# Two kinds of small TensorE products moved within the steps of a fused decoder, one of them into another PSUM bank

## The chip, the core and the metric

The kernel runs on one core of a Trainium2 chip, as one launch. The metric is the time of the launch on the device in microseconds (us); less is better. Before the change three runs took 360.64, 361.13 and 362.26 us, so the median is 361.13 us.

## What is computed

Two decoder layers over x of 16 x 64 tokens with 128 features, all in float32. After each of the six blocks the input is added and a layer norm without weights is made:

```python
x = _layernorm(x + L0_attn(x))          # 16 heads of 8, rotary positions, causal, biases
x = _layernorm(x + L0_xattn(x, ctx))    # 16 heads of 8, keys and values from ctx, mask, biases
x = _layernorm(x + L0_ffn(x))           # 8 experts of 512, the best 2 of each token, silu(g) * u
x = _layernorm(x + L1_attn(x))          # 16 heads of 64, no mask
x = _layernorm(x + L1_xattn(x, ctx))    # 16 heads of 8, mask
x = _layernorm(x + L1_ffn(x))           # ternary weights, 512 wide, gelu, layer norm, projection
# one attention: q, k, v = x @ Wq, src @ Wk, src @ Wv, cut into heads
#   att = softmax(q k^T / sqrt(d) + mask);  out = (att v) @ Wo
```

## The kernel before

The 1024 tokens are eight tiles of 128 rows (two sequences of 64). The three attentions with heads of 8 are objects of class Narrow: a0 (self-attention with rotary positions, "rope"), a1 and a2 (cross-attentions). The attention with heads of 64 is `wide`, the last block is `fc`, the experts are `moe`. The tiles stand in two streams: `pre` is a0's eight and then a1's eight (places 0 to 15), `post` is wide's, a2's and fc's (places 0 to 23; a2 has 8 to 15). Between the streams lie a drain written out by hand, in which the last tiles of a1 end while the experts' weights are turned, and the experts' 23 blocks.

Four functions write each engine's program, one step j after the other, and a step works on several tiles at once, each at another stage of its way. In a step of narrow tiles TensorE does, in this order: the scores of tile j-2 (`s_pe`, L539 and L547 or L550), the transpose of the normalized y of tile j-5 (`y_pe`, L582), the projections of k and q of tile j (`qk_pe`, L511), the value projection of tile j-2 (`v_pe`, L523), the transposes of P, the exponentials, of tile j-3 (`t_pe`, L429), the output projection of tile j-5 (`o_pe`, L586), P's products with the values of tile j-4 (`va_pe`, L566), and the transpose of the finished X of tile j-6 (`x_pe`, L371). I call the tile that is transposed at the end of step j "X of step j". TensorE has no other order than this one: each product waits by semaphores for its inputs and for the readers of the PSUM bank that it writes.

Three shapes of the array are used, and the profile prints them with each product: 128\*128 (the whole array: projections and transposes), 128\*64 (the value projection and P's products with values) and 64\*64 (the scores).

The other engines in such a step: ScalarE (ACT) copies y (`y_act`, L632 or L630), q (`qk_act`), the values (`v_act`, L620, two copies), P transposed (`pt_act`, L438, two copies), makes the exponentials (`exp_act`, L419) and copies X transposed into XT (`x_act`, L376). VectorE (DVE) makes the row maximum (L403) and the difference (L413), the residual and its statistics (L388, L324, L326), k, and then the reciprocals and ysb (L676, L680). GpSimd (POOL) spreads k into blocks (KB, L690), makes the norm's root (L331, L333), applies it (L337) and adds a bias (L716).

Banks of PSUM that matter here: B_S (two, scores), B_PT (two, P transposed), B_Y (P's products with values in columns 0 to 287, and the value projection in 384 to 511), B_OX (y transposed, output projection, X transposed), B_K and B_Q (k and q of a tile, 128 columns each). No product is written into a bank while an engine reads another part of it; the waits see to that.

At the first block of the experts TensorE first does 32 transposes whose result is not used (`turn_over`, L1521), then the first block that the DMA queue of SyncE (SP) has loaded into XG (`block_pe`, L1527). At the start of `post`, VectorE combines the experts' outputs of a pair of tiles (`combine`) and applies their norm (`apply`, L1742), and TensorE turns them (`turn_pe`, L1752).

## Time and profile before

| what | value |
|---|---|
| median of three runs | 361.13 us |
| the profiled execution, its own time | 360.73 us |
| its span (first to last instruction) | 358.7 us |
| busy in the span: PE | 321.0 us (89%) |
| PEld, DVE, ACT, POOL | 262.9 us, 231.4 us, 182.5 us, 203.0 us |
| mean granted TensorE clock, share of full speed | 0.983 |

The page of the profile gives, for each engine, its busy time, and then the chain of work that ended last, followed back from the last instruction. The timeline lists instructions in the order of time, with neighbours of one kind merged: start, the time from the first start to the last end, the line, what is written and read, the shape of the array for products, and the count (one product of float32 is two entries). In brackets stands how long the engine had been idle before, and what released it. Because products overlap in the pipeline, it is the distance from one start to the next that tells what a group costs TensorE, and not its printed length.

### The profile page before, as it was taken

To read this page: it belongs to the slowest core of one execution; us is meant where nothing else is said; L and a number is where in the kernel's file an instruction comes from. 1 tells how busy PE (TensorE), PEld (TensorE's weight loads), DVE (VectorE), ACT (ScalarE), POOL (GpSimd) and SP (SyncE) were. 2 spreads that over 40 slices of the span, in tenths; PEclk is the share of its full clock that TensorE was granted. 3 is DMA by queue.
4 is the path that set the end of the run, shared out by engine and by line. 5 is a ranking of instruction groups with operands and counts; after the bars stand their busy time and mean duration, and the time that the engine had idled before them with its cause. 6 is when DMAs were issued, how large, how long until landed. Compare 5 with 4: busy or idle time off the path is not lost.

```text
span 358.7 us, 10785 instructions
## 1 busy us (share of the span) xinstructions
PE 321.0 (89%) x4214; PEld 262.9 (73%) x4214; DVE 231.4 (65%) x554; ACT 182.5 (51%) x384; POOL 203.0 (57%) x289
## 2 busy tenths in 40 slices
PE   2969999999888799999994689999999799999993
PEld 2647667777677799999994567788888577767673
DVE  2698987887876033583343479765556667877685
ACT  2457667776658732333322234445444466667651
POOL 2756998887677335553314776432122564576784
PEclk9998999999999999999999699999999999999998
DMA  6799999100011111111101110000000000000001
GB/s 190 219 308 246 296 324 322 32 2 3 16 38 47 59 41 50 46 45 51 41 22 36 40 38 24 2 4 2 2 4 2 3 4 3 2 2 2 4 22 37
DMA packets 37052, 23.55 MB, mean 66 GB/s; under 512 B 4228, under 2 KB 34956, under 8 KB 36876
## 3 DMA queue, kind: packets, MB, share of 16 engines
q1 hardware_dynamic: 35692, 20.16, 19.9%
q0 software_dynamic: 1024, 2.10, 2.0%
q8 instruction: 34, 0.56, 0.7%
q10 hardware_dynamic: 288, 0.62, 0.5%
q14 instruction: 14, 0.11, 0.1%
HBM read 15.13 MB, written 7.73 MB: 64 GB/s over the span
## 4 chain that ended last, share of the span: by engine, by line
PE 74%; DVE 12%; issue 4%; ACT 4%; POOL 3%; DMA 2%; SPq 1%; POOLq 0%; ACTq 0%; DVEq 0%
PE banks L429 8%; PE banks L801 8%; PE banks L1555 6%; PE banks L1586 6%; PE banks L1563 6%; PE banks L566 5%; PE banks L539 5%; PE banks L845 4%; PE banks L813 4%; PE banks L511 3%; PE banks L861 2%; PE banks L523 2%; PE banks L827 2%; PE banks L1026 2%; ACT WALL L1353 2%
## 5 line engine op out<-in xcount | busy, mean ns | idle before, releaser
L690 POOL TENSOR_TENSOR KB<-KT,cst 128x512 f32<-128x512 f32 x48 | 49.3, 1048 | 8.1 <-DVE KT L650 5.8
L438 ACT ACTIVATE PT<-banks 128x512 f32<-128x512 f32 x64 | 34.8, 595 | 24.4 <-PE banks L429 23.2
L403 DVE TENSOR_REDUCE mx<-banks 128x16 f32<-128x1024 f32 x32 | 38.6, 1206 | 11.7 <-PE banks L550 10.1
L1578 DVE TENSOR_TENSOR PT<-banks,PR 128x512 f32<-128x512 f32 x23 | 15.9, 691 | 40.2 <-PE banks L1563 35.9
L1543 POOL COPY U<-WALL 128x1024 f32 x21 | 21.9, 1042 | 34.8 <-PE banks L1563 34.7
L877 ACT ACTIVATE U<-banks 128x512 f32<-128x512 f32 x44 | 26.1, 597 | 29.7 <-PE banks L801 14.4
L331 POOL TENSOR_SCALAR ve<-mv 128x1 f32<-128x1 f32 x40 | 9.2, 231 | 49.4 <-DVE mv L326 49.0
L429 PE MATMUL banks<-cst,PR 128*128 128x128 f32 x256 | 35.4, 282 | 0.6 <-POOL PR L906 0.6
L419 ACT ACTIVATE PR<-PR 128x1024 f32<-128x1024 f32 x32 | 33.8, 1058 | 3.6 <-DVE PR L413 3.3
L801 PE MATMUL banks<-XT,WQKV 128*128 128x128 f32 x256 | 32.1, 286 | 0.4 <-ACT XT L1758 0.4
L801 PEld LDWEIGHTS banks<-XT,WQKV 128*128 128x128 f32 x256 | 30.6, 199 | 1.1 <-ACT XT L1758 0.7
L429 PEld LDWEIGHTS banks<-cst,PR 128*128 128x128 f32 x256 | 28.1, 143 | 4.3 <-POOL PR L906 1.5
L413 DVE TENSOR_TENSOR PR<-banks,mx 128x1024 f32<-128x1024 f32 x24 | 29.4, 1224 | 0.8
L539 PE MATMUL banks<-KB,QS 64*64 64x512 f32 x192 | 27.0, 627 | 3.2 <-DVE PR L413 2.2
L566 PE MATMUL banks<-VB,PT 128*64 128x18 f32 x768 | 26.7, 212 | 0.0
L566 PEld LDWEIGHTS banks<-VB,PT 128*64 128x64 f32 x768 | 24.3, 138 | 3.0 <-issue 0.5
L1712 POOL DMA_INDIRECT KB<-routed_rows,pos x16 | 15.9, 993 | 16.4 <-DMA routed_rows<-YS 12.3
L333 POOL TENSOR_TENSOR rstd<-ve,half 128x1 f32<-128x1 f32 x40 | 23.2, 579 | 3.3
L1586 PE MATMUL banks<-WALL,PT 128*128 x184 | 24.4, 276 | 0.6 <-DVE YS L1594 0.6
L1555 PE MATMUL banks<-XGT,U 128*128 128x128 f32 x184 | 24.5, 276 | 0.5 <-ACT XGT L1533 0.5
L906 POOL TENSOR_TENSOR PR<-PR,rs 128x1024 f32<-128x1024 f32 x8 | 15.2, 1904 | 17.1 <-DVE rs L916 17.0
L1563 PE MATMUL banks<-XGT,U 128*128 128x128 f32 x184 | 24.3, 275 | 0.0
(192 smaller groups left out, 727.0 us busy)
## 6 DMA issues: line engine op xcount, KB each, us to landing
routed_rows<-zero SPq DMA_DIRECT2D x1, 4544.0 KB, 19.7
WALL<-in_L_ffn_wg_dram SPq DMA_DIRECT2D x8, 256.0 KB, 5.5
WALL<-in_L_ffn_wu_dram SPq DMA_DIRECT2D x8, 256.0 KB, 5.7
WALL<-in_L_ffn_wd_dram SPq DMA_DIRECT2D x8, 256.0 KB, 6.1
U<-in_L_attn_W_qkv_dram SPq DMA_DIRECT2D x1, 1536.0 KB, 22.2
XG<-routed_rows SPq DMA_DIRECT2D x23, 64.0 KB, 1.8
routed_rows<-YS SPq DMA_DIRECT2D x23, 64.0 KB, 1.6
cst<-shape_constants ACTq DMA_DIRECT2D x1, 537.0 KB, 4.4
```

The costliest lines, as they stand in the source:

```text
L403: dve.tensor_reduce(mx[:, n % 2, :], s, AX.X, ALU.max).then_inc(self.max.sem, 1)
L413: dve.tensor_tensor(PR[:, n % 2, :].rearrange("q (h k) -> q h k", k=SEQ), s, bc(mx[:, n % 2, :], 2, SEQ), ALU.subtract).then_inc(self.sub. ...
L419: act.activation(p, p, ACT.Exp, scale=self.scale).then_inc(self.exp.sem, 1)
L429: t = pe.transpose(PS[:, B_PT + m, P * (r % 4):P * (r % 4 + 1)], PR[:, n % 2, P * r:P * (r + 1)], ident)
L438: act.activation(PT[:, n % 2, 4 * m:4 * m + 4, :].rearrange("p r q -> p (r q)"), PS[:, B_PT + m, :], ACT.Copy).then_inc(self.pt.sem, 1)
L539: pe.matmul(PS[q, B_S + g, :], QS[f, n % 3, q], KB[f, n % 2, b].rearrange("p h k -> p (h k)"), start=True, stop=False)
L566: m = pe.matmul(PS[64 * b:64 * b + 64, B_Y, w * r:w * (r + 1)], PT[:, n % 2, r, 64 * b:64 * b + 64], VB[:, n % 3, r, b].rearrange("p a e - ...
L690: pool.tensor_tensor(KB[:, n % 2, b], bc(KT[:, n % 2, b, :], 1, 8), bc(cst[:, C_HEAD:C_HEAD + 8], 2, SEQ), ALU.mult).then_inc(self.kb.sem, 1)
L801: m = pe.matmul(PS[:, bank, P * k:P * (k + 1)], WQKV[:, f // 2, P * u:P * (u + 1)], XT[:, P * i:P * (i + 1)], start=True, stop=True)
L1555: m = pe.matmul(PS[:, j % 2, P * c:P * (c + 1)], WE[:, j % 3, 0, P * c:P * (c + 1)], XGT[:, j % 3, :], start=True, stop=True)
L1563: m = pe.matmul(PS[:, 2 + j % 2, P * c:P * (c + 1)], WE[:, j % 3, 1, P * c:P * (c + 1)], XGT[:, j % 3, :], start=True, stop=True)
L1586: m = pe.matmul(PS[:, 7, 0:P], HT[:, j % 2, c, :], WALL[:, e, 2, P * c:P * (c + 1)], start=(c == 0), stop=(c == CH - 1))
```

## The change

It has four parts.

1. **Value projection.** For a narrow tile that has a narrow tile two places behind it in the stream (`late_v`: places 0 to 13 of `pre`, a2's places 8 to 13 of `post`) v_pe is written into bank B_Q, columns 128 to 255, and stands right ahead of va_pe, after o_pe. It waits for q's copy of the tile of this step (`after2 ... qk_read`), because that copy reads the same bank, and the projection of q three tiles on waits for v's copy. va_pe no longer waits for v's copy. On ACT v_act comes after pt_act. The first ranking product of the experts (`rank_pe`, in B_Q) waits for the v of place 13.
2. **X.** For a0's tiles, a1's first and a2's places 8 to 13 (`late_x`) the transpose of X is taken from the end of a step and stands in the next step between s_pe and y_pe; its copy on ACT comes after y_act. y_pe no longer waits for the copy of X two tiles back, and o_pe does.
3. **turn_over** does 25 transposes in place of 32.
4. **apply** for tiles 2 to 5 of the experts' norm comes on DVE after max_dve, ahead of the copies of wide's projections, and not after them.

```diff
 qk_pe:
                 for bank, w, src, s in ((B_K, 1, self.src, self.k_mm), (B_Q, 0, XT, self.q_mm)):
+                    if s is self.q_mm and job.ago(3) and job.ago(3).late_v:
+                        for r in job.ago(3).v_read():
+                            pe.wait_ge(*r)
...
+            def v_at(self, job, rows, b):
+                bank, c = (B_Q, P) if job.late_v else (B_Y, 384)
+                return PS[rows, bank, c:c + P] if b is None else PS[rows, bank, c + 64 * b:c + 64 * b + 64]
 v_pe:
-                if job.ago(3):
+                if job.late_v:
+                    pe.wait_ge(*job.after2.stage.qk_read(job.after2.i)[1])
+                elif job.ago(3):
                     pe.wait_ge(*job.ago(3).y_read())
...
-                        m = pe.matmul(PS[64 * a:64 * a + 64, B_Y, 384 + 64 * b:448 + 64 * b],
+                        m = pe.matmul(self.v_at(job, slice(64 * a, 64 * a + 64), b),
 va_pe:
-                if job.after2:
+                if job.after2 and not job.after2.late_v:
 y_pe:
-                if job.ago(2) and not (self is a1 and i >= 6):
+                if job.ago(2) and not job.ago(2).late_x and not (self is a1 and i >= 6):
 o_pe:
+                if job.ago(2) and job.ago(2).late_x:
+                    pe.wait_ge(*job.ago(2).x_read())
...
+            def late_v(self):
+                return isinstance(self.stage, Narrow) and self.after2 is not None
+            def late_x(self):
+                return self.late_v and not (self.stage is a1 and self.i >= 1)
 stream_pe:
                 if y:
+                    if y.ago(2) and y.ago(2).late_x:
+                        y.ago(2).stage.x_pe(pe, y.ago(2))
                     y.stage.y_pe(pe, y)
...
-                if a:
+                if a and not a.late_v:
                     a.stage.v_pe(pe, a)
...
                 if y:
                     y.stage.o_pe(pe, y)
+                if a and a.late_v:
+                    a.stage.v_pe(pe, a)
                 if v and not first_v and not v.stage.wide:
                     v.stage.va_pe(pe, v)
...
                 for x in turned(tiles, j):
-                    x.stage.x_pe(pe, x)
+                    if not x.late_x:
+                        x.stage.x_pe(pe, x)
 stream_dve:
                     v.stage.max_dve(dve, v)
+                if tiles is post and j in (2, 3):
+                    for g in (2 * j - 2, 2 * j - 1):
+                        moe.apply(dve, g)
 Routed.pe:
-                self.turn_over(pe, 32)
+                self.turn_over(pe, 25)
 post_dve:
-            if not late and j in (2, 3):
-                for t in (2 * j - 2, 2 * j - 1):
-                    moe.apply(dve, t)
```

TensorE in a step of a1, before. L539 and L550 are the scores, L371 is X of the step before or of this one.

```order
L539 MATMUL banks<-KB,QS 64x512 x4
L550 MATMUL banks<-mrb,fills 64x512 x4
L582 MATMUL banks<-cst,ysb 128x128
L511 MATMUL banks<-CT,WT 128x128
L511 MATMUL banks<-XT,WT 128x128
L523 MATMUL banks<-WT,CT 64x64 x4
L429 MATMUL banks<-cst,PR 128x128 x8
L586 MATMUL banks<-WT,yT 128x128
L566 MATMUL banks<-VB,PT 64x18 x16
L371 MATMUL banks<-cst,X 128x128
```

The same step now (the scores have the lines L548 and L559, y L591, k and q L514, v L532, the output projection L597, P's products with values L575).

```order
L548 MATMUL banks<-KB,QS 64x512 x4
L559 MATMUL banks<-mrb,fills 64x512 x4
L371 MATMUL banks<-cst,X 128x128
L591 MATMUL banks<-cst,ysb 128x128
L514 MATMUL banks<-CT,WT 128x128
L514 MATMUL banks<-XT,WT 128x128
L429 MATMUL banks<-cst,PR 128x128 x8
L597 MATMUL banks<-WT,yT 128x128
L532 MATMUL banks<-WT,CT 64x64 x4
L575 MATMUL banks<-VB,PT 64x18 x16
```

The value projection has moved behind the output projection, and X ahead of y; the array changes its shape before each of L582, L523, L429, L566, L371 and L539 in the first list, and before L371, L532 and L548 in the second.

TensorE in `post` from step 11 on, where the last two tiles of `wide` meet a2: the end of L845, wide's output projection (128\*64), to the next scores, before.

```order
L845 MATMUL banks<-U 64x128
L429 MATMUL banks<-cst,PR 128x128 x8
L371 MATMUL banks<-cst,X 128x128
L539 MATMUL banks<-KB,QS 64x512 x4
L550 MATMUL banks<-mrb,fills 64x512 x4
```

And now.

```order
L429 MATMUL banks<-cst,PR 128x128 x8
L532 MATMUL banks<-WT,CT 64x64 x4
L371 MATMUL banks<-cst,X 128x128
L548 MATMUL banks<-KB,QS 64x512 x4
L559 MATMUL banks<-mrb,fills 64x512 x4
```

Here the value projection, which stood ahead of L845 and had its shape, has moved between two groups of 128\*128. This is so in steps 10 and 11 of `post`.

VectorE in step 2 of `post`, before: L403 and L409 are the maximum and the difference of wide's first tile, L877 copies of its projections, L1742 is `apply`, L1722 the start of `combine`.

```order
L403 TENSOR_REDUCE mx<-banks 128x16
L409 TENSOR_TENSOR PR<-banks,mx 128x2x8x64
L877 COPY U<-banks 128x512 x2
L1742 TENSOR_SCALAR X<-R,mv,rstd 128x128 x2
L1722 SCALAR_TENSOR_TENSOR R<-KB,pk,X 128x128
```

And now.

```order
L403 TENSOR_REDUCE mx<-banks 128x16
L409 TENSOR_TENSOR PR<-banks,mx 128x2x8x64
L1777 TENSOR_SCALAR X<-R,mv,rstd 128x128 x2
L888 COPY U<-banks 128x512 x2
L1757 SCALAR_TENSOR_TENSOR R<-KB,pk,X 128x128
```

The two `apply` have changed places with the two copies, and stand directly behind the difference.

## Rows read from the trace of the kernel before

**Rows 1.** Page, part 4: the chain that ended last, by engine.

```profile
PE 74%; DVE 12%; issue 4%; ACT 4%; POOL 3%; DMA 2%; SPq 1%; POOLq 0%; ACTq 0%; DVEq 0%
```

**Rows 2.** Timeline of PE, one step of a1: start, length, line, shapes, count.

```profile
60.95 1.09 PE L539 MATMUL banks<-KB,QS 64*64 64x512 f32 x8
61.85 0.40 PE L550 MATMUL banks<-mrb,fills 64*64 64x512 bf16 x4
62.18 0.33 PE L582 MATMUL banks<-cst,ysb 128*128 128x128 f32 x1
62.35 0.39 PE L511 MATMUL banks<-CT,WT 128*128 128x128 f32 x2
62.57 0.39 PE L511 MATMUL banks<-XT,WT 128*128 128x128 f32 x2
62.89 0.45 PE L523 MATMUL banks<-WT,CT 128*64 128x64 f32 x8
63.27 1.09 PE L429 MATMUL banks<-cst,PR 128*128 128x128 f32 x8
64.20 0.39 PE L586 MATMUL banks<-WT,yT 128*128 128x128 f32 x2
64.52 1.11 PE L566 MATMUL banks<-VB,PT 128*64 128x18 f32 x32
65.56 0.33 PE L371 MATMUL banks<-cst,X 128*128 128x128 f32 x1
65.82 1.09 PE L539 MATMUL banks<-KB,QS 64*64 64x512 f32 x8
```

**Rows 3.** Timeline of PE: a step without X, and a long run of one shape.

```profile
34.16 1.11 PE L566 MATMUL banks<-VB,PT 128*64 128x18 f32 x32
35.20 1.09 PE L539 MATMUL banks<-KB,QS 64*64 64x512 f32 x8
...
112.91 5.00 PE L1348 MATMUL banks<-cst,WALL 128*128 128x128 f32 x44
```

**Rows 4.** Timeline of all engines in the step of rows 2.

```profile
62.29 1.23 DVE L403 TENSOR_REDUCE mx<-banks 128x16 f32<-128x1024 f32 x1 [0.88 <-PE banks L550]
...
63.00 0.37 ACT L609 ACTIVATE QS<-banks,qkb 128x128 f32<-128x128 f32 x1
...
65.00 1.06 ACT L419 ACTIVATE PR<-PR 128x1024 f32<-128x1024 f32 x1
...
65.61 0.23 POOL L331 TENSOR_SCALAR ve<-mv 128x1 f32<-128x1 f32 x1 [0.52 <-DVE mv L326]
```

**Rows 5.** Timeline of DVE, a step of a0 (rope).

```profile
43.37 1.23 DVE L413 TENSOR_TENSOR PR<-banks,mx 128x1024 f32<-128x1024 f32 x1
...
44.71 0.29 DVE L388 TENSOR_TENSOR R<-banks,XR 128x128 f32<-128x128 f32 x1
```

**Rows 6.** Timeline of PE at the first block of the experts; and XG's landings.

```profile
119.68 3.68 PE L1521 MATMUL banks<-cst 128*128 128x128 f32 x32 [1.77 <-ACT WALL L1353]
123.20 0.27 PE L1527 MATMUL banks<-cst,XG 128*128 128x128 f32 x1
```

```profile
DMA to landing us min/median/max: 1.7/1.8/3.1
```

**Rows 7.** Timeline of all engines, steps 2 and 3 of post.

```profile
213.81 0.59 DVE L1742 TENSOR_SCALAR X<-R,mv,rstd 128x128 f32<-128x128 f32 x2
...
214.50 0.41 PE L1752 MATMUL banks<-cst,X 128*128 128x128 f32 x2 [1.35 <-issue]
...
222.27 1.09 PE L429 MATMUL banks<-cst,PR 128*128 128x128 f32 x8 [0.63 <-POOL PR L906]
```

**Rows 8.** Timeline of PE, step 11 of post, and of DVE in step 12.

```profile
298.46 0.29 PE L845 MATMUL banks<-WOUT,U 128*64 128x128 f32 x1 [0.56 <-ACT U L877]
```

```profile
304.82 1.23 DVE L413 TENSOR_TENSOR PR<-banks,mx 128x1024 f32<-128x1024 f32 x1
```

**Rows 9.** Timeline of PE, step 19 of post.

```profile
334.35 0.30 PE L582 MATMUL banks<-cst,ysb 128*128 128x128 f32 x1 [0.54 <-issue]
```

More of the change, by code:

```diff
@@ L620, in v_act @@
                     m = act.activation(VB[rows, n % 3, :, :, a, 0:DH].rearrange("p r b d -> p b r d"),
-                                       PS[rows, B_Y, 384:512].rearrange("p (b r d) -> p b r d", b=2, d=DH), ACT.Copy)
+                                       self.v_at(job, rows, None).rearrange("p (b r d) -> p b r d", b=2, d=DH), ACT.Copy)
                 m.then_inc(self.v_ready.sem, 1)
@@ L1218, in stream_act @@
                     y.stage.y_act(act, y)
+                    if y.ago(2) and y.ago(2).late_x:
+                        y.ago(2).stage.x_act(act, y.ago(2))
                 b, q, v = at(tiles, j), at(tiles, j - 1), at(tiles, j - 2)
@@ L1229, in stream_act @@
                     v.stage.vw_copies(act, 0, v)
-                    v.stage.v_act(act, v)
+                    if not v.late_v:
+                        v.stage.v_act(act, v)
                 extra(act, j, False)
@@ L1234, in stream_act @@
                     t.stage.pt_act(act, t)
+                if v and v.late_v:
+                    v.stage.v_act(act, v)
                 hidden = v and isinstance(v.stage, Ternary)
@@ L1244, in stream_act @@
                 for x in turned(tiles, j):
-                    x.stage.x_act(act, x)
+                    if not x.late_x:
+                        x.stage.x_act(act, x)
                 extra(act, j, True)
@@ L1405, in rank_pe @@
                     pe.wait_ge(s_rt, 3)
+                    for s in pre[-3].v_read():
+                        pe.wait_ge(*s)
                 else:
```

2 lines of the change are left out of this document (added).

## The prediction, made before the changed kernel ran

> **What bounds the kernel now.** I read the chain that ended last first: 74% of the span is PE [rows 1]. So the question is which parts of the program PE sets, and for what it pays there. The timeline of PE answers it for a step of a1 [rows 2]: from 60.95 to 65.82 there is no bracket with idle time; one step takes 4.87 us, and the steps of a1 and a2 repeat it. The reader is to look there at the starts, and to compare them with what the same products cost in a row. 44 transposes of shape 128\*128 take 5.00 us, the last of them some 0.28, so 0.11 each [rows 3]. In rows 2 the eight of L429 take 63.27 to 64.20, 0.93 in place of 0.88; the two of L586 0.32 in place of 0.22; the second pair of L511 0.32 where the first took 0.22; X (L371) 0.26 in place of 0.11; y (L582) 0.17 in place of 0.11. The excess stands only where the shape of the array changes: some 0.10 behind the last product of the old shape and some 0.05 at the first of the new one. A semaphore is not its cause: L511's second operand, L429 and L586 all wait for something else than their forerunner, and between L429 and L586 there is none. A second reading gives the same without a model: with X between L566 and the next scores it is 1.30 us from 64.52 to 65.82 [rows 2], without it 1.04, from 34.16 to 35.20 [rows 3]; so an X alone among other shapes costs 0.26, and in a run of its own shape 0.11.
>
> Of the other engines I want the slack in the same step [rows 4]. DVE was idle for 0.88 before its maximum, POOL for 0.52 before the norm's root. So PE could be faster by about 0.5 before POOL sets the pace, and by 0.9 before DVE does.
>
> **The price of a step after the change.** A step has six changes of shape now and three then. (a) v joins L566: L511 to L566 took 3.21 us (62.35 to 65.56). Now L511 takes 0.44 and L429 0.88 without a change, L586 0.32 with the change behind it, v 0.28 (its 0.38 less the exit of 0.10), and L566 1.02, since v pays the entry. That is 2.94, or 0.27 less. (b) X joins y: 0.15. Together 0.42, and a step takes 4.45. POOL's 0.52 leaves 0.10, DVE's 0.88 leaves 0.46: PE stays the bound, POOL closely behind.
>
> The Trainium skill, page "TensorEngine Tiling (Array Packing)", Key Properties, says that changing the tiling mode drains the engine, and "TensorE: Matmul & The Clock Gate", Single matmul latency, puts a drain at about 128 cycles. At 2.4 GHz that would be an estimated 0.05 us for each change, 0.16 per step and not 0.42, and the forecast would be about 358 us (4.45 us of gain from (a) and (b) become 1.7). The rows above have 0.15 per change, and they decide.
>
> **New waits.** v waits for q's copy on ACT. That copy took 0.37 and ended at 63.37, 2.42 us into the step [rows 4]; the copy of X, of the same size, now comes ahead of it, so it ends at 2.8 at the latest. v now stands behind L429 and L586, at 1.23 (scores) + 0.06 + 0.11 (X) + 0.11 (y) + 0.44 + 0.88 + 0.32 = 3.15: it would wait for nothing, with 0.35 to spare. Queued behind it are L566 and the next scores, for which DVE waits. On ACT v's copies only change places with P's, so that the exponentials, which ended at 66.06 and so 5.1 into the step [rows 4], end 0.37 later for X's sake, at 5.5; L429 needs them 1.95 into the next step, that is at 6.4. o_pe's wait for X's copy (over at 2.45) ends before its turn (2.83). The three waits cost nothing; without that cover each costs what it overruns, in every step.
>
> **The sum**, in stretches.
>
> *a0's steps 4 to 7.* Here DVE has the rotary work too, and PE waits for it. The residual (44.71) starts 0.11 after the difference has ended (43.37 + 1.23) [rows 5], because it waits for PE's L586. With v out of the way L586 comes 0.4 earlier, and 0.1 of that is gained in each of steps 6 and 7; X doesn't matter there. Ahead of them step 4 and step 5 are PE's and POOL's, and I take 0.25 for v's part, less than one step's (a). Sum 0.4, bounds 0 and 0.9.
>
> *pre, from step 8 to step 16.* Part (a) holds in steps 8 to 15, 8 x 0.27 = 2.2. Part (b) holds at seven borders of steps, since a1's tiles 1 to 7 keep their X at the end: 7 x 0.15 = 1.05. Sum 3.2. If POOL can't follow at 4.45 the bound is its own 4.87 - 0.52 = 4.35 and some jitter; at the worst half of this stays, 1.6. The drain behind it is a chain from these tiles through DVE, ACT and POOL, all of which start from PE's last scores, so it moves as a whole and keeps the gain.
>
> *turn_over.* 32 transposes take 119.68 to 123.20, 0.11 each; seven fewer are 0.77, if the first block is there at 122.43. Its load was issued at 120.55 and a landing takes 1.7 to 1.8 us in the median [rows 6]: 122.3. I take 0.77; with the longest landing of 3.1 it would be 0.
>
> *apply.* Now the two norms (0.59 on DVE) stand where DVE would else wait for PE's products, and not between the last copy and combine. The chain goes combine, POOL's root, two gathers, POOL's shares, L429, which waited 0.63 for it [rows 7]. combine starts earlier by the two norms, 0.59, less their overlap with the copy ahead: 0.4. PE's own wait of 1.35 before L1752 goes too, but PE then waits longer at 222: nothing of it counts. Bounds 0 and 0.6.
>
> *Steps 10 to 12 of post.* Here the change costs. v stood ahead of L845, with its shape, and in the time that L845 waits for ACT anyway (0.56 [rows 8]). Now it stands between two groups of 128\*128: 0.24 for its four pairs of products, and 0.15 for the change of shape on either side, 0.53 in each of steps 10 and 11 (the exact starts in rows 2 give 0.10 + 0.38 + 0.05). Step 12 saves 0.28 again by (a), so that 0.8 is left if PE alone sets these steps. But DVE's difference of step 12 ends only at 306.05 (304.82 + 1.23) [rows 8], the scores of the next step wait for it, and its chain starts at L845 of step 11, ahead of the second 0.53. Half of the 0.8 would hide there; I take a loss of 0.45, bounds 0.2 and 1.1.
>
> *Steps 13 to 19 of post.* (a) in steps 13, 14 and 15, 0.8; (b) at the three borders of 14/15 to 16/17, 0.45. From step 18 on the scores are fc's, of shape 128\*128, and (b) gives nothing. In step 19 y waited 0.54 [rows 9], because X's copy two tiles back stood behind the table load and the gelu on ACT; y no longer waits for it, but the transposes behind y still wait for that gelu, so I take 0.35, bounds 0 and 0.5. Sum 1.6.
>
> 0.4 + 3.2 + 0.77 + 0.4 - 0.45 + 1.6 = 5.9. The profiled execution of 360.73 becomes 354.8. It was 0.4 faster than the median of the three, and from the median 361.13 it is **355.2 us**.
>
> **Rivals.** *POOL becomes the bound.* For it: only 0.10 is left of its 0.52, and the order of its work (root, norm, bias, KB) is a chain that starts from DVE's statistics. Against it: its blocks are needed only one step after they are made. If a step settles at 4.65, half of the 4.45 us that (a) and (b) bring (3.2 + 1.25) is lost: 357.4.
>
> *The gaps are not the shape's.* Then (a) and (b) give nothing, and the rest, 0.77 + 0.4 + 0.35 less 0.1 or 0.2, gives 359.8. Against it: the two readings of X, 1.30 and 1.04.
>
> *The change doesn't reach the end.* The drain or the start of post could be set by something that doesn't move with PE's steps, such as a DMA. Then up to 2 us are given back: 356.9. The drain's waits name DVE, ACT and POOL, so I hold this for small.
>
> *Slower: v waits for q's copy.* ACT's row y, X, q, P, v, exponentials would have to put q's copy later than v's turn. It starts to cost at 0.35 of delay and eats the step's gain from 0.35 + 0.42 = 0.77 us on. If the copy came 1.0 us late in each of some 18 steps, each would lose 0.2: 361.13 + 3.6 - 1.1 (the other terms) = 363.6. Against it: ACT's exponentials end about one us into the next step, while y's copy can't start before 1.6.
>
> **Chances.** Forecast with its bounds 0.74; POOL's pace 0.11; gains given back 0.07; gaps not the shape's 0.04; slower 0.04. The range takes in POOL's pace and, on the other side, all terms at their better ends (0.5 in a0, 0.2 in apply, 0.25 at steps 10 to 12, 0.15 at step 19, and some of each step): 353.6 to 357.6. About 0.5% (1.8 us) is what a measurement of this kernel can tell from no change: faster by more 0.92, within it 0.04, slower by more 0.04.
>
> **What would show it.** In the timeline of PE a step of a1 of 4.45 us without idle; 0.11 for each of X and y in a row; 1.04 or so from L575 to the scores. DVE idle for 0.46 and POOL for 0.1 before the same rows; a wait of PE on DVE's k, on KB or in front of L532 would show the rivals. L1527 2.75 us after the first of 25 transposes. L429 in step 3 of post still waiting for POOL. Two longer steps, 10 and 11, in post. The largest doubt is POOL's 0.10.

## The result, and the profile after

The changed kernel takes 358.16 us (median of 5 runs, 356.87 to 358.33), the kernel before 361.72 in the 5 runs beside it: a ratio of 0.9893, 95% interval 0.9864 to 0.9922. The change makes the kernel faster by about 1%, which is 3.6 us, where 5.9 were forecast; 358.2 lies outside the range of 353.6 to 357.6. In the later batches of runs the kernel before had medians of 360.95 to 361.12, against which the gain is 2.8 to 3.0 us. The profiled execution took 358.16 with a span of 356.2, and that of the kernel before 360.73 with 358.7: 2.5 us in the traces. The terms of the forecast are compared with this pair of traces.

Two rows of the page answer to [rows 1] and to the granted clock of the kernel before. First the chain that ended last, then PE's granted clock in 40 slices of the span (9 is 90% or more):

```profile
PE 69%; DVE 14%; ACT 5%; issue 5%; POOL 2%; DMA 2%; SPq 1%; POOLq 0%; ACTq 0%; DVEq 0%
PEclk9989999999999999999997699999999999999999
```

PE still sets most of the chain, five points less than before. The 7 and the 6 stand where the kernel before has a single 6: there the kernel runs at a lower clock for longer.

**A step of a1.** The timeline of PE (start, length, line, shapes, count), in the place of [rows 2]:

```profile
63.66 1.09 PE L548 MATMUL banks<-KB,QS 64*64 64x512 f32 x8
...
64.90 0.33 PE L371 MATMUL banks<-cst,X 128*128 128x128 f32 x1
65.07 0.27 PE L591 MATMUL banks<-cst,ysb 128*128 128x128 f32 x1
65.17 0.39 PE L514 MATMUL banks<-CT,WT 128*128 128x128 f32 x2
...
66.50 0.39 PE L597 MATMUL banks<-WT,yT 128*128 128x128 f32 x2
66.81 0.45 PE L532 MATMUL banks<-WT,CT 128*64 128x64 f32 x8
67.09 1.06 PE L575 MATMUL banks<-VB,PT 128*64 128x18 f32 x32
68.09 1.29 PE L548 MATMUL banks<-KB,QS 64*64 64x512 f32 x8
```

63.66 to 68.09 is 4.43 us, for which 4.45 was forecast; y takes 0.10 behind X, and the scores start 1.00 after L575. But the next L548 takes 1.29 in place of 1.09, and the step that begins with it 4.63. Between the first and the last step of a1 steps of 4.43 and 4.63 alternate. POOL in the same place (it answers to the last row of [rows 4]):

```profile
61.17 0.46 POOL L727 TENSOR_TENSOR XR<-X,rowb 128x128 f32<-128x128 f32 x1
61.58 2.04 POOL L701 TENSOR_TENSOR KB<-KT,cst 128x512 f32<-128x512 f32 x2
63.90 0.23 POOL L331 TENSOR_SCALAR ve<-mv 128x1 f32<-128x1 f32 x1 [0.27 <-DVE mv L326]
...
65.79 0.46 POOL L727 TENSOR_TENSOR XR<-X,rowb 128x128 f32<-128x128 f32 x1
66.21 2.05 POOL L701 TENSOR_TENSOR KB<-KT,cst 128x512 f32<-128x512 f32 x2
68.33 0.23 POOL L331 TENSOR_SCALAR ve<-mv 128x1 f32<-128x1 f32 x1
```

KB's second half ends at 66.21 + 2.05 = 68.26, after the start of the long L548 at 68.09; at 63.62 it was 0.04 ahead of the short one at 63.66. In the short row the first four of L548's products start within 0.02 us; in the long one the two that need KB's second half start 0.22 behind the other two, at 68.31. POOL's idle time is 0.27 in one step and none in the next, where [rows 4] have 0.52.

**The start of post.** Stretches of 3 us: busy time of PE, its weight loads, DVE, ACT and POOL, then the granted clock (0.84 in the first row of the changed kernel). First three of the kernel before, then five of the changed kernel:

```profile
196.00:199.00 3.00, 0.00 (x0) 0.00 (x0) 1.26 (x5) 0.00 (x0) 2.00 (x4) 0.56 0.19 44
199.00:202.00 3.00, 2.22 (x9) 1.96 (x10) 1.36 (x5) 0.28 (x1) 2.51 (x4) 0.50 0.13 30
202.00:205.00 3.00, 3.00 (x24) 3.00 (x24) 0.94 (x2) 1.58 (x3) 2.50 (x3) 0.80 0.17 44
```

```profile
190.00:193.00 3.00, 1.16 (x8) 0.97 (x8) 0.96 (x5) 0.00 (x0) 2.39 (x3) 0.84 0.17 46
193.00:196.00 3.00, 0.45 (x1) 0.18 (x1) 1.83 (x7) 0.04 (x1) 2.19 (x4) 0.50 0.16 41
196.00:199.00 3.00, 2.71 (x12) 2.72 (x13) 0.97 (x4) 0.78 (x2) 2.39 (x5) 0.50 0.17 46
199.00:202.00 3.00, 3.00 (x16) 3.00 (x16) 0.45 (x1) 0.84 (x3) 2.39 (x3) 0.50 0.15 41
202.00:205.00 3.00, 2.23 (x73) 1.96 (x72) 1.88 (x6) 0.68 (x2) 1.27 (x3) 0.95 0.18 46
```

At 0.50 the clock is at the lower level, 1.2 GHz. The five rows make (0.16 + 3 x 0.50 + 0.05) x 3 us / 0.5 = 10.3 us at that level, from 192.0 to 202.3; the three of the kernel before make 6.8, from 196.4 to 203.2. The fall comes 0.6 us (0.9 in the kernel before) after PE's last product, in a wait of 4.07 us for the experts' first X. That X is turned at 195.47, so that 6.8 us of the low clock lie on work of PE; in the kernel before (199.41) it is 3.8. The first 32 products of L812 take 6.69 us there; the kernel before needed 5.24 for its 32 of L801.

**The norms.** Timeline of DVE, POOL and PE in steps 3 and 4 of post, beside [rows 7]:

```profile
217.44 2.11 DVE L1777 TENSOR_SCALAR X<-R,mv,rstd 128x128 f32<-128x128 f32 x2
219.47 1.28 DVE L888 COPY U<-banks 128x512 f32<-128x512 f32 x2
...
217.28 1.91 POOL L917 TENSOR_TENSOR PR<-PR,rs 128x1024 f32<-128x1024 f32 x1
...
219.25 1.09 PE L429 MATMUL banks<-cst,PR 128*128 128x128 f32 x8 [1.45 <-POOL PR L917]
...
229.73 0.29 PE L856 MATMUL banks<-WOUT,U 128*64 128x128 f32 x1 [0.97 <-DVE U L888]
```

The two norms that took 0.59 in [rows 7] take 2.11: they begin 0.16 after POOL's shares and end 0.36 (one norm) after POOL has ended at 219.19. The copies behind them are late, and L856 waits 0.97 for them.

**Step 12 of post.** ACT and PE:

```profile
303.94 0.57 ACT L631 ACTIVATE VB<-banks 64x128 f32<-64x128 f32 x2 [0.61 <-PE banks L532]
304.54 1.06 ACT L419 ACTIVATE PR<-PR 128x1024 f32<-128x1024 f32 x1
305.62 0.28 ACT L376 ACTIVATE XT<-banks 128x128 f32<-128x128 f32 x1
...
306.04 0.30 PE L591 MATMUL banks<-cst,ysb 128*128 128x128 f32 x1 [0.66 <-ACT XT L376]
```

v's copy waits for v, the exponentials wait behind it, the wide tile's X behind them, and y for X.

### The profile page after: what moved, and what is told of

Read it like the earlier page. It is cut to its first block, busy times and chain, and to the rows that moved or that the text cites. A ratio compares the mean times of both kernels' runs of the same rounds, so it can differ in the third digit from the quotient of the medians.

```text
span 356.2 us, 10773 instructions
## 1 busy us (share of the span) xinstructions
PE 316.5 (89%) x4207; PEld 262.3 (74%) x4207; DVE 232.6 (65%) x554; ACT 182.4 (51%) x384; POOL 202.9 (57%) x289
## 4 chain that ended last, share of the span: by engine, by line
PE 69%; DVE 14%; ACT 5%; issue 5%; POOL 2%; DMA 2%; SPq 1%; POOLq 0%; ACTq 0%; DVEq 0%
PE banks L812 7%; PE banks L429 6%; PE banks L1590 6%; PE banks L1621 6%; PE banks L1598 6%; PE banks L548 6%; PE banks L575 5%; PE banks L856 4%; PE banks L824 3%; PE banks L514 3%; PE banks L872 2%; PE banks L532 2%; DVE mx L403 2%; ACT WALL L1386 2%; PE banks L838 2%
## 5 line engine op out<-in xcount | busy, mean ns | idle before, releaser
L403 DVE TENSOR_REDUCE mx<-banks 128x16 f32<-128x1024 f32 x32 | 38.6, 1206 | 8.7 <-PE banks L559 7.3
L429 PE MATMUL banks<-cst,PR 128*128 128x128 f32 x256 | 34.2, 277 | 1.5 <-POOL PR L917 1.5
L812 PE MATMUL banks<-XT,WQKV 128*128 128x128 f32 x256 | 33.6, 294 | 0.4 <-ACT XT L1793 0.4
L812 PEld LDWEIGHTS banks<-XT,WQKV 128*128 128x128 f32 x256 | 32.0, 207 | 1.1 <-ACT XT L1793 0.7
L429 PEld LDWEIGHTS banks<-cst,PR 128*128 128x128 f32 x256 | 28.8, 143 | 3.9 <-POOL PR L917 2.3
L548 PE MATMUL banks<-KB,QS 64*64 64x512 f32 x192 | 28.1, 634 | 2.9 <-DVE PR L413 2.2
L575 PE MATMUL banks<-VB,PT 128*64 128x18 f32 x768 | 26.0, 210 | 0.0
L575 PEld LDWEIGHTS banks<-VB,PT 128*64 128x64 f32 x768 | 24.4, 138 | 1.2 <-issue 0.3
```

The lines of the kernel that those rows point to most:

```text
L403: dve.tensor_reduce(mx[:, n % 2, :], s, AX.X, ALU.max).then_inc(self.max.sem, 1)
L429: t = pe.transpose(PS[:, B_PT + m, P * (r % 4):P * (r % 4 + 1)], PR[:, n % 2, P * r:P * (r + 1)], ident)
L548: pe.matmul(PS[q, B_S + g, :], QS[f, n % 3, q], KB[f, n % 2, b].rearrange("p h k -> p (h k)"), start=True, stop=False)
L575: m = pe.matmul(PS[64 * b:64 * b + 64, B_Y, w * r:w * (r + 1)], PT[:, n % 2, r, 64 * b:64 * b + 64], VB[:, n % 3, r, b].rearrange("p a e - ...
L812: m = pe.matmul(PS[:, bank, P * k:P * (k + 1)], WQKV[:, f // 2, P * u:P * (u + 1)], XT[:, P * i:P * (i + 1)], start=True, stop=True)
```

## Where the lead is won and lost

For each kernel I take its lead over the kernel before at fixed instructions of PE and write down by how much it grew or fell between them. The start times of the same instruction are simply subtracted; the times in the head are those of the kernel before. A column hardly depends on what came earlier, so profiles whose clock differed at another place can be compared: the seven kernels that do the same in a1 have 2.72 to 2.77 there. Each row is one profile.

| kernel | y of a1, 47.56 to 86.55 | first X of the experts to wide scores, 199.41 to 206.34 | wide scores, to 235.22 | steps 10 to 13, 284.32 to 307.45 | 13 to 18, to 329.38 | to the end, 348.34 | lead there |
|---|---|---|---|---|---|---|---|
| changed kernel | 2.72 | -1.45 | 0.08 | -1.16 | 1.12 | 0.00 | 2.53 |
| e1, v alone | 2.40 | -0.30 | 0.08 | -1.15 | 0.87 | 0.00 | 2.61 |
| e2, X alone | 1.07 | -0.27 | 0.09 | 0.01 | 0.51 | 0.00 | 2.10 |
| e3, bias ahead of root | 3.44 | 0.05 | 0.10 | -1.16 | 1.50 | -0.02 | 5.04 |
| e4, norms back | 2.77 | -1.37 | 0.00 | -1.16 | 1.18 | 0.00 | 3.53 |
| e5, changed, kept busy | 2.72 | 1.52 | -0.36 | -1.16 | 1.17 | 0.00 | 6.02 |
| e6, before, kept busy | 0.00 | 1.52 | 0.00 | 0.01 | 0.00 | 0.00 | 2.72 |
| e7, v late from tile 3 | 2.72 | -0.10 | 0.05 | 0.00 | 1.17 | 0.00 | 4.71 |
| e12, v late from tile 2 | 2.76 | -1.41 | 0.08 | -0.32 | 1.18 | -0.06 | 3.61 |
| e13, first pair of norms | 2.74 | 0.05 | 0.53 | -1.17 | 1.14 | 0.00 | 4.53 |
| e14, norms back, kept busy | 2.77 | 1.52 | 0.00 | -1.17 | 1.18 | 0.00 | 6.58 |
| e9, four costs away | 3.44 | -0.45 | 0.02 | 0.02 | 1.51 | -0.03 | 5.33 |
| e10, the same, kept busy | 3.44 | 1.52 | -0.01 | 0.01 | 1.53 | -0.02 | 7.45 |
| e11, kept busy twice | 3.45 | 1.58 | 0.02 | -0.24 | 1.53 | -0.02 | 7.24 |
| e15, and one pair of norms | 3.15 | 1.54 | 0.11 | 0.01 | 1.53 | -0.02 | 7.31 |

What a row lacks to its last column was won ahead of 47.56 (in the changed kernel 0.56, elsewhere -0.01 to 1.53, mostly by a lower clock early on, see below) and in turn_over (0.79 in the changed kernel, 0.77 forecast, 0.6 to 0.8 elsewhere); up to 0.2 moved among the experts, and 0.9 in e11 and e15 (below). Two numbers stand out: e11's -0.24 in steps 10 to 13 and e15's 3.15 in a1 where e11 has 3.45. Each is one hold of PE of 0.2 to 0.3 us within a group of products (L856 and L575) that does not come again in the other profile; no run shows its cause.

## The experiments

**The parts alone.** e1 keeps v's new place and puts X back; e2 keeps X's and puts v back.

```diff
 def late_x(self):                       # e1
-    return self.late_v and not (self.stage is a1 and self.i >= 1)
+    return False
```

```diff
 def late_v(self):                       # e2 (late_x keeps its old condition)
-    return isinstance(self.stage, Narrow) and self.after2 is not None
+    return False
```

> The changed kernel with X back at the end of the step; only the value projection stays late. Theory (the time lies at the changes of shape, and the second half of KB sets every other step of a1): steps of a1 become 4.87 - 0.27 = 4.60 and even, since KB's second half, 9.0 us after the start two steps back, is then ahead of 2 x 4.60 = 9.2. The lead over the kernel before at y of tile 16 of pre becomes 0.56 + 8 x 0.27 = 2.7 (it was 3.28 in the changed kernel); steps 14 to 17 of post lose 0.45. With the rest as it is: about 359.1. Rival (the gaps are not the shape's, X's place is worth nothing): 358.2, with steps as in the changed kernel. Rival (POOL's total of work sets the pace of the changed kernel): the lead at tile 16 stays at about 3.2.

> The changed kernel with the value projection back at its old place in its old bank; only X stays beside y. Theory: steps of a1 4.87 - 0.15 = 4.72, the lead over the kernel before at tile 16 of pre about 1.05 (7 borders of 0.15); post has no longer steps 10 and 11 (1.16 less lost there), but no 0.27 in steps 13 to 15 (0.8). Against the changed kernel 2.2 less before the experts and 0.4 more behind them: about 360.0. If the new chain of the wide tile's X copy behind the exponentials (step 13 of post) is X's doing and not v's, 0.3 of the loss stays: 360.3. Rival (shape changes cost nothing): lead at tile 16 zero, 361.

e1 took 358.48 us (ratio 0.9934, 0.9913 to 0.9955), e2 359.40 (0.9950, 0.9921 to 0.9979). In a1 v alone brings 2.40 in eight steps, 0.30 each, and its steps are even at 4.57 or 4.58; X alone brings 1.07 at seven borders, 0.15 each. So both prices of the prediction hold, and neither is nothing. Together they would be 3.47 and the changed kernel has 2.72: 0.75 go where both meet. The loss of steps 10 to 13 is v's alone (-1.15 with it, 0.01 without).

**A direct price of the shape change.** e8 puts six groups of small products in the place of turn_over in the kernel before: `full` is the transpose that stood there (128\*128), `half` and `quarter` are products of shape 128\*64 and 64\*64 from the same operand.

```diff
-for _ in range(n):
-    pe.transpose(PS[:, B_Y, 0:P], ident, ident)
...
+for order in ((full,), (half,), (full, half), (quarter,), (full, quarter), (full,)):
+    for _ in range(16):
+        for product in order:
+            product()
```

> The kernel before, whose 32 transposes ahead of the experts are replaced by six groups: 16 of 128*128, 16 of 128*64, 16 pairs that alternate between both, 16 of 64*64, 16 pairs that alternate between 128*128 and 64*64, 16 of 128*128; read from PE's timeline alone. Theory (0.10 us behind the last product of the old shape and 0.05 ahead of the first of the new one, 0.15 for each change): a pair that alternates costs its two products in a row and 0.3, so the 16 pairs about 4.8 us more than the two groups. Rival (a change costs only a drain of 0.05): 1.6 us more. Rival (a change costs nothing, the gaps are something else's): the same.

Timeline of PE (a product of 32-bit numbers that isn't a transpose counts twice):

```profile
118.62 1.94 PE L1521 MATMUL banks<-cst 128*128 128x128 f32 x16 [1.73 <-ACT WALL L1353]
120.49 2.08 PE L1524 MATMUL banks<-cst 128*64 128x64 f32 x32
122.50 0.33 PE L1521 MATMUL banks<-cst 128*128 128x128 f32 x1
122.76 0.33 PE L1524 MATMUL banks<-cst 128*64 128x64 f32 x2
...
130.78 2.08 PE L1527 MATMUL banks<-cst 64*64 64x64 f32 x32
132.79 0.33 PE L1521 MATMUL banks<-cst 128*128 128x128 f32 x1
...
136.38 0.36 PE L1521 MATMUL banks<-cst 128*128 128x128 f32 x1
```

In a row 16 of each cost 1.87 and 2.01 us; the 16 pairs cost 130.78 - 122.50 = 8.28. The rest, 4.40 us for 32 changes, is 0.14 for each. With 64*64, seven pairs cost 136.38 - 132.79 = 3.59, in a row 7 x (0.117 + 0.126) = 1.70: 1.89 for 14 changes, 0.14 again. The rival of 0.05 would have made 1.6 us. That bears out the 0.15 of the prediction. The Trainium skill, page "TensorEngine Tiling (Array Packing)", Key Properties, has the drain at a change of mode and no price for it. The Trainium skill, page "TensorE: Matmul & The Clock Gate", Single matmul latency, has the 128 cycles from which 0.05 us was estimated; e8's 0.14 is almost three times that.

**Why the steps alternate.** e3 changes the order of POOL's work, not its amount.

```diff
+for x in turned(tiles, j):
+    x.stage.bias_pool(pool, x)
 for r in summed(tiles, j):
     r.stage.rsqrt_pool(pool, r)
-for x in turned(tiles, j):
-    x.stage.bias_pool(pool, x)
```

> The changed kernel, but POOL adds the next stage's bias (XR, 0.42 us) ahead of the norm's root in place of behind it, so that KB comes 0.42 earlier after DVE's statistics; POOL's total work is the same. Theory (a chain from the scores over DVE's maximum, the difference, the statistics, POOL's root, norm and KB back to the scores two steps on makes every other step of a1 0.20 long): all steps 4.43, four products of L548 start together in each of them, 4 x 0.2 = 0.8 us less: 357.4. Rival (POOL is simply full, its 4.42 us of work per step are the pace): the mean step stays at 4.53 and the time at 358.2. Rival (DVE or ACT make the long steps): the same, 358.2.

355.33 us (0.9847, 0.9819 to 0.9876). PE and POOL:

```profile
63.50 1.09 PE L548 MATMUL banks<-KB,QS 64*64 64x512 f32 x8
...
67.92 1.09 PE L548 MATMUL banks<-KB,QS 64*64 64x512 f32 x8
...
61.20 2.04 POOL L701 TENSOR_TENSOR KB<-KT,cst 128x512 f32<-128x512 f32 x2
63.20 0.45 POOL L727 TENSOR_TENSOR XR<-X,rowb 128x128 f32<-128x128 f32 x1
```

KB is ready at 63.24, 0.26 ahead of the scores, every L548 takes 1.09, every step but a1's last 4.42 or 4.43. POOL does the same work per step (4.36 us in the changed kernel: 59.27 to 63.90 less 0.27 of idle time); its total is not the pace, the chain from DVE's statistics over root, norm, bias and KB to the scores was. The eight steps bring 3.44, the sum of both parts (3.47), and steps 13 to 18 bring 0.38 more. That makes 1.1 us of the 2.8 by which the median fell; 1.50 of the rest is the half clock, which cost little in its profile and is no merit of the order.

**The half clock.** e5 and e6 add 32 transposes that nobody reads where PE waited for the experts' first X, e5 to the changed kernel, e6 to the one before.

```diff
 fc.means_pe(pe)
 pe.wait_ge(*fc.bias.at(1))
+self.turn_over(pe, 32)
 self.turn_pe(pe, (0,))
```

> The changed kernel with 32 transposes more (of the identity, into a free bank, read by nobody) between the means of fc and the first X of the experts, where PE waited 4.07 us. Theory (1.45 us of the forecast went to a longer stretch of half clock at the start of post, 10.24 us after 6.83, that begins while PE is idle there): the granted clock stays at 1.00 from 190 to 205, the first 32 products of L812 take about 3.5 where they took 6.7, and the lead over the kernel before at the wide tile 0's scores is 3.9 + 1.7 and more in place of 2.49: about 355.2, and less spread between runs. Rival (the half clock comes from something else than PE's idle time, for instance from load ahead of it): the stretch stays or moves, 358.2. Rival (the 32 transposes reach into the path): L1787 starts later than 4.07 after the means, 358.5.

> The kernel before with the same 32 transposes at the same place. Theory: its own half-clock stretch of 6.83 us goes as well, so that the kernel before gains what half of it cost, about 1.5 to 3 us less what the waits behind it take back: 358.5. The difference to the changed kernel with the transposes is then free of this clock and shows the change alone: 3.94 at the first X, +0.08 (norms), -1.16 (steps 10 to 13), +1.12 (to the end): 4.0 us. Rival (the clock has nothing to do with the idle time): 361.1.

e5 took 356.84 us (354.79 to 359.20; ratio 0.9897, 0.9840 to 0.9953), e6 359.02 (0.9948, 0.9932 to 0.9965). The stretches of e5 and its PE:

```profile
193.00:196.00 3.00, 2.30 (x19) 1.88 (x18) 1.59 (x6) 0.28 (x1) 2.18 (x4) 1.00 0.09 25
196.00:199.00 3.00, 3.00 (x29) 2.96 (x27) 0.94 (x2) 1.79 (x3) 2.68 (x4) 1.00 0.16 44
...
190.57 3.66 PE L1556 MATMUL banks<-cst 128*128 128x128 f32 x32
194.56 0.33 PE L1788 MATMUL banks<-cst,X 128*128 128x128 f32 x1 [0.33 <-DVE X L1778]
195.26 3.84 PE L812 MATMUL banks<-XT,WQKV 128*128 128x128 f32 x32 [0.37 <-ACT XT L1794]
```

The clock stays at 1.00 and L812's 32 products take 3.84. In each of e5, e6, e10 and e14 the lead grows by 1.52 there, in e11 and e15 by 1.58 and 1.53. So the half clock costs the kernel before 1.5 us and the changed kernel 1.52 + 1.45 = 2.97, and with the transposes in PE's wait it doesn't come at this place in any of the six profiles. (In e11 and e15 it comes a little earlier, see below.)

How much it costs isn't the change's doing. e4, e7, e12 and e13 have the changed kernel's program up to this point, and by their rows the low clock lasts 6.8 us in each. What counts is how much of it lies on PE's work between the first X and wide's scores: 3.8 us in the kernel before, 3.7 to 4.0 in e3, e7 and e13 (0.05, -0.10, 0.05 of lead), 4.4 in e1 and e2 (-0.30, -0.27), 4.7 in e9 (-0.45), 6.6 and 6.7 in e4 and e12 (-1.37, -1.41), 6.8 in the changed kernel (-1.45). In e4 and e12 the clock falls only when the first X is there (194.4 for 194.5, 195.2 for 195.3). The lead falls by just under half of what lies there beyond 3.8. Within the runs of the changed kernel two (356.87 and 356.95, mean clock 0.983) lie 1.3 us under the other three (0.980).

With both kernels kept busy the change is worth 6.02 - 2.72 = 3.3 us where the two profiles without it have 2.53; 4.0 was expected. It gets back the 1.45, but starts a1 with 0.2 less of lead and loses 0.4 more by the norms (below). e5's run times did not follow: 355.2 and less spread were expected. Part of that lies outside the span from the first to the last instruction: its four runs have 3.1, 3.6, 3.8 and 2.1 us between time and span, where the changed kernel has 2.0; the spans are 352.7 to 355.4. The rest goes with the mean clock (0.981 to 0.999); at which places it was low in the slower runs was not seen.

**v in steps 10 to 12 of post.** e7 leaves v of a2's tiles 0 to 2 at its old place, e12 that of tiles 0 and 1.

```diff
 def late_v(self):
-    return isinstance(self.stage, Narrow) and self.after2 is not None
+    return isinstance(self.stage, Narrow) and self.after2 is not None and not (self.stage is a2 and self.i <= 2)
```

In both `late_x` keeps its old condition, so that X stays where the change has put it.

> The changed kernel, but in a2 the value projections of tiles 0, 1 and 2 stay at their old place (steps 10, 11 and 12 of post). Theory (v between two full groups costs 0.53 in steps 10 and 11, and in step 12 its copy comes ahead of the exponentials): the lead at y of step 13 is the one at the wide tile 5's L856 to within 0.1, where it fell by 1.16; steps 13 to 19 are as in the changed kernel: 357.0. Rival (the fall comes with the passage from v's old bank to the new one wherever it is): the loss moves to step 13: 358.2.

> The changed kernel with the value projections of a2's tiles 0 and 1 at their old place, those from tile 2 on late. Tells apart what steps 10 and 11 and what step 12 lose of the 1.16. Theory: in steps 10 and 11 v stands between two full groups (0.53 each, of which 0.26 was regained, and the step's end is hidden in part by DVE), in step 12 v's copy on ACT comes ahead of the exponentials and puts off the copy of the wide tile's X that y waits for, 0.3 to 0.4: lead at y of step 13 about 0.35 below that at the wide tile 5. Rival (all of it comes from v between the two full groups): no fall at all in this kernel.

e7 took 356.56 us (0.9890, 0.9859 to 0.9921), e12 357.08 in its one run. The lead falls by 1.16 with all three late, by 0.32 with tile 2 alone, not at all with none. So steps 10 and 11 cost 0.84 and step 12, by its new chain on ACT, 0.32. X's new place is no part of it, as e2 has said.

**The norms.** e4 takes all four back, e13 only the pair of step 3, e14 all four with PE kept busy.

```diff
 def post_dve(dve, j, late):             # e4, e14 (e13: j == 3 alone)
+    if not late and j in (2, 3):
+        for t in (2 * j - 2, 2 * j - 1):
+            moe.apply(dve, t)
```

The early place behind max_dve is taken out for the same steps.

> The changed kernel with the experts' norms (apply of tiles 2 to 5) back behind DVE's copies in steps 2 and 3 of post. Theory (the early place puts two norms on DVE beside POOL's shares, and DVE is held up until POOL has ended): the pair takes 0.59 again in place of 2.11, the first L856 of step 4 doesn't wait 0.97 for DVE's U, L429 of step 3 waits for POOL about as long as in the kernel before; the move's 0.5 at L429 and the 0.45 lost at L856 cancel: 358.2 within 0.2. Rival (the 0.45 at L856 has another cause, such as the half clock): the wait of 0.97 stays and the 0.5 goes: 358.7. Rival (the collision costs more than is seen): 357.7.

> The changed kernel with the norms of the experts' tiles 4 and 5 (step 3 of post) back behind DVE's copies, those of tiles 2 and 3 (step 2) still early. Theory (the 0.5 that the lead rises by L429 of step 3 is the work of step 2's pair, and the 0.45 that it falls by the first L856 is the work of step 3's pair, which runs beside POOL's shares): the rise stays and the fall goes; step 3's pair takes 0.59 in place of 2.11, no wait of 0.97 at L856. With the half clock as in the changed kernel 0.45 less than it. Rival (both belong to step 3's pair): no rise and no fall, as with all four norms back. Rival (the fall is the half clock's): it stays.

> The changed kernel with the 32 transposes that keep PE busy and all four norms in their old place. With the transposes alone the lead over the kernel before with the same transposes went 3.66 (first X), 3.74 (L429's step), 3.30 (wide tile 3). Theory (at full clock L429 doesn't wait for the norms' chain any more, so that the early place gives 0.08 there and costs 0.44 behind): here the lead stays at 3.6 to 3.7 through all three, so the move as a whole costs 0.36. Rival (the 0.36 has another cause): 3.66, 3.66, 3.30 again.

e4 took 357.16 us (0.9900, 0.9873 to 0.9926; its profile is 0.9 ahead at 47.56 already, at full clock there), e13 356.16, e14 355.08, the latter two in one run each. Between the wide scores and 235.22 the move of all four is worth 0.08, that of the first pair alone 0.53, and with all four back it is 0.00. In the changed kernel the lead had risen by 0.53 up to L429 and fallen by 0.45 at L856, and e13 keeps the rise and has no fall. DVE and PE in e13:

```profile
217.10 0.91 DVE L1777 TENSOR_SCALAR X<-R,mv,rstd 128x128 f32<-128x128 f32 x2
...
227.75 0.32 PE L856 MATMUL banks<-WOUT,U 128*64 128x128 f32 x1 [0.53 <-ACT XT L1793]
```

Its POOL's shares end at 215.74 + 1.92 = 217.66, and the pair that begins at 217.10 ends 0.35 after that, at 218.01; late, but there is nothing behind it that PE needs soon. With PE kept busy the move of all four costs 0.36 (e5), and with the norms in their old place nothing is lost (e14: its lead over e6 is 3.85 at the first X and at the fourth wide tile).

The second pair runs into POOL's shares in five of the profiles: it takes 2.11 us in the changed kernel and in e3, 2.53 in e5, 1.31 in e15 and 0.91 in e13, in place of 0.59, and always ends one norm (0.34 to 0.36) after POOL. POOL's own instruction takes its usual 1.91 or 1.92. In e5 the norms begin first:

```profile
213.58 2.53 DVE L1778 TENSOR_SCALAR X<-R,mv,rstd 128x128 f32<-128x128 f32 x2
213.85 1.92 POOL L917 TENSOR_TENSOR PR<-PR,rs 128x1024 f32<-128x1024 f32 x1
```

The Trainium skill, page "SBUF — State Buffer", section "SBUF: two separate sides", says that VectorE (in an instruction that uses both ports, or with two inputs in SBUF) and GpSimd share a pair of ports as an exclusive lock that whoever starts first holds for its whole instruction. That one waits until the other has ended is what the rows show; that the first to start wins is not, for in e5 the norm that began 0.27 us ahead of POOL is held all the same. No run shows whether these norms use both ports. A reader of that page could still have seen this cost ahead of the change.

**Everything together.** e9 has e3's order, all four norms back, v late from tile 3 on, and X of a2's tile 5 at the end of step 19 again; e10 adds the 32 transposes, e11 18 more in step 3 of pre, e15 moves the first pair of norms of e11 forward.

```diff
 if j in (2, 3) and late:                # e11, e15
     weights.pe(pe, [j - 2])
+if j == 3 and late:
+    moe.turn_over(pe, 18)
```

> The changed kernel with four of its costs taken away: POOL's bias ahead of the root, the experts' norms back in their old place, the value projections of a2 late only from tile 3 on, and X of a2's tile 5 back at the end of step 19 (it came ahead of y in step 20, where L597 waited for its copy and the lead fell by 0.49). Theory, from the leads of the earlier runs: 3.86 at tile 16 of pre, +0.77, -1.4 for the half clock as in the changed kernel, 0 in steps 10 to 13, +1.1 in 13 to 18, +0.71 in step 19, 0 in step 20: a lead of 5.1 at the end, 355.6; with the shorter half-clock stretch that the run with the bias ahead of the root had, 354.2. Rival (step 19's 0.71 comes from what step 20 then gives back, whatever X does there): 0.4 to 0.5 more.

> The same with 32 transposes more ahead of the experts' first X. Theory: no half clock at the start of post, so 1.5 us more of lead there than the kernel before has, and the norms at their old place keep the 0.36 that the run with the transposes alone lost between the third and the fourth wide tile's scores: lead 4.6 + 1.5 + 1.1 + 0.7 = 7.9, 352.9. Rival (without the half clock the norms' place doesn't matter, the 0.36 goes anyway): 353.3. Rival (the half clock comes at another place instead, in some runs): the spread between the runs stays at 2 to 4 us and the median is near the previous one.

> The same with 18 transposes more behind the weights' transposes of step 3 of pre, where PE waited 2.18 us for DVE's difference ahead of the scores at 24.55 and the granted clock fell to 0.63 in the next 3 us (the profiles that had 1.00 there reached the first y 0.6 and the second 0.9 us earlier). Theory: the clock stays at 1.00 there in every run, 0.9 us less in those runs that had the fall: a median of 352.2. Rival (PE has slack there, as DVE sets these steps): no difference to the kernel with one group of transposes.

> The kernel with four costs taken away and kept busy twice (353.34 us in its runs), with step 2's pair of norms early again. Theory: at full clock the pair gives 0 to 0.1 at L429 and costs nothing behind, so 353.3. Rival (it gives the 0.5 that it gave under the half clock): 352.8. Rival (this pair too meets work of POOL and is held up): 353.7.

| kernel | us, median | runs | ratio, 95% |
|---|---|---|---|
| e9 | 355.19 | 353.91 to 355.53 | 0.9820 (0.9789 to 0.9851) |
| e10 | 353.58 | 352.33 to 355.75 | 0.9787 (0.9748 to 0.9826) |
| e11 | 353.34 | 352.75 to 354.44 | 0.9779 (0.9748 to 0.9810) |
| e15 | 353.63 | 352.94 to 355.16 | 0.9795 (0.9757 to 0.9833) |

All four beat both kernels; e10, e11 and e15 can't be told apart, and are some 7.5 us or 2.1% ahead of the kernel before. Two expectations went astray. X of tile 5 was to save the 0.49 that step 20 loses; the gain of step 19 is given back all the same (-0.03 in the column to the end), the last 0.3 of it at the last X (336.26), which waits for POOL's norm (L337, to 336.20). POOL began that norm's root at 334.41, behind the bias at 333.99, though DVE's statistics had ended at 333.87: e9 has the bias ahead of the root. So the gain is lost to another wait there than in the changed kernel, and no run shows whether it could be kept.

e11's second group was to keep the clock up in step 3 of pre. Its granted clock from 24 to 27 is 1.00 where the changed kernel has 0.63, and its lead at 47.56 is 1.04 where e10's is 0.23. But the profiles of e4, e5, e6 and e14, which lack that group, have 1.00 there too, and are 1.1 to 1.5 ahead at 47.56; so the profile alone doesn't show that the group did it; the mean clock of e11's six runs (0.992 to 1.000, e10's 0.981 to 0.997) speaks for it. And at the first X e10 and e11 have the same lead (4.42 and 4.36): in e11's profile the clock is at the lower level from 188.8 to 192.2, over the eight products ahead of the 32 transposes and the first third of these. The eight take 2.08 us in place of 1.16 in e10; PE had no longer wait ahead of them than 1.25. e15 has the same from 189.0 on.

```profile
189.06 2.08 PE L1009 MATMUL banks<-FCT,PT 128*128 128x128 f32 x8 [1.25 <-DVE FCT L1000]
189.00:192.00 3.00, 2.94 (x13) 2.94 (x14) 0.99 (x6) 0.00 (x0) 2.39 (x3) 0.50 0.22 63
```

e15's first pair of norms brings 0.11 at full clock between the wide scores and 235.22, as its theory had it, which is too little for its run times to show.

## Right and wrong, step by step

The sum of the prediction against the leads in the two traces:

| term | forecast | measured |
|---|---|---|
| up to step 8 | 0.4 | 0.56 |
| pre, steps 8 to 16 | 3.2 | 2.72 |
| turn_over | 0.77 | 0.79 |
| drain and experts | 0 | -0.13 |
| half clock at the start of post | not seen | -1.45 |
| norms | 0.4 | 0.08 |
| steps 10 to 13 of post | -0.45 | -1.16 |
| steps 13 to 18 | 1.25 | 1.12 |
| step 19 and the tail | 0.35 | 0.00 |
| sum | 5.9 | 2.5 |

**What bounds the kernel, and the price of a change of shape** were right: 0.14 by e8, 0.30 and 0.15 per step by e1 and e2, a step of 4.43.

**The sum, pre:** the step that failed is "its blocks are needed only one step after they are made". The four quadrants of L548 start together, so KB's second half is needed at the first product. POOL's slack of 0.10 was worked out from its idle time in one step, where the chain through it is two steps long: twice 4.43 and a little, 8.88 us, were there for a chain of 9.0 (from the scores at 54.61 to KB's end at 63.62). The rival "POOL becomes the bound" had named this: the order of POOL's work as a chain. What it had wrong is the size, since only every other step is long (4.53 in the mean, not 4.65), and POOL's amount of work fits. The term came out 0.48 short; e3 shows that the wait cost 0.72, as v's part was 0.30 in a step and not 0.27.

**The sum, the clock:** the largest miss, and no term of the prediction. The row of the granted clock stood on the page before with its 6, and the half clock was taken as given. In the changed kernel's profile it lies on 6.8 us of PE's work in place of 3.8, and by their mean clock in three of its five runs, which is chance as far as the runs show. 1.45 of the 3.4 us between 5.9 and 2.5 are this.

**The sum, apply:** "the two norms stand where DVE would else wait" was checked against DVE's own queue, not against POOL's shares beside it. The first pair brought its 0.5, the second took 0.45 (e13). The 0.5 came only in profiles with the half clock at the start of post; without it the same pair brought 0.11 (e15). Why is open.

**The sum, steps 10 to 12:** the mechanism was right and the term too small. I let half of the loss hide and took 0.45; the bound of 1.1 was the truth, 1.16. ACT's queue in step 12 was left out: v's copy ahead of the exponentials holds up X of the wide tile (0.32, e12).

**New waits:** those of a1 cost nothing, as was said. **Steps 13 to 18** came out at 1.12 for 1.25, by the same alternation of 0.2. **Step 19** gained 0.49 by y (334.35), and what follows gave it back, in e9 too, there by a wait for POOL: a wait of PE went, and others came behind it. The forecast took a gain at one product for a gain at the end.

**Up to step 8:** 0.56 for 0.4, but 0.38 of it was there at the first y already, where the low clock of 3.4 us near 25 lies on other instructions than in the kernel before. e5 and e6 have no low clock there: their leads are equal at the first y, and e5 is 0.37 ahead at 47.56. So the term was right.

## What to carry to other kernels

Count the changes of the array's shape in a loop that PE sets, and put products of one shape together: each change costs 0.14 us here, for both pairs of shapes that were tried. When a step gets shorter, follow every chain that reaches over two steps, and ask when its last input is needed by the first of the products that run side by side. Look at the row of the granted clock before you make a sum, and try to keep PE at work where it waits long: 32 transposes of nothing were worth 1.5 us to the kernel before in its trace, more than half of what the change brought in its own. Where another engine's instruction is to be moved, look at what runs beside its new place, and not only at its own queue.

## What the hardware showed

- The granted clock fell with PE at work too. In e8 PE was busy for all of the 3 us from 133 on, alternating between shapes (the busy time takes in what the changes of shape cost), and the clock went from 1.00 to 0.59 and 0.50:

```profile
133.00:136.00 3.00, 3.00 (x19) 1.95 (x18) 0.00 (x0) 0.00 (x0) 0.00 (x0) 1.00 0.00 0
136.00:139.00 3.00, 3.00 (x13) 1.72 (x13) 0.00 (x0) 0.00 (x0) 0.00 (x0) 0.59 0.00 0
139.00:142.00 3.00, 3.00 (x13) 1.77 (x12) 0.00 (x0) 0.00 (x0) 0.00 (x0) 0.50 0.00 0
```

- The same program meets a lower clock at one place in one run and not in the next: near 25 us it falls to 0.5 for 3.4 us in the changed kernel, e7, e12 and e13 and not in e4 and e5, which do the same up to there. At the first y the latter are 0.6 us ahead.
- DVE's tensor_scalar from SBUF to SBUF stood still behind POOL's tensor_tensor: 2.11 and 2.53 us for 0.59, the second although it had begun first.
- A run's time is not its span and a constant: 2.0 us lie outside in most profiles, 3.0 in e14's, and 2.1 to 3.8 in the four runs of e5.
